# First self attention of a decoder: next batch's rows turned in the tail of the softmax loop, output projection in three rounded products

## What is computed

```python
x = _layernorm(x + _L0_attn_ref(x, Wq, bq, Wk, bk, Wv, bv, Wo, bo), axis=-1)

def _L0_attn_ref(x, Wq, bq, Wk, bk, Wv, bv, Wo, bo):
    q, k, v = (to_heads(x @ W + b) for W, b in ((Wq, bq), (Wk, bk), (Wv, bv)))   # 8 heads of 64
    scores = jnp.einsum('bdsh,bdth->bdst', q, k) / SCALE
    weights = jax.nn.softmax(scores, axis=-1)
    feats = jnp.einsum('bdst,bdth->bdsh', weights, v)
    return feats @ Wo + bo
```

## Time and profile before

| | |
|---|---|
| median of 3 executions | 2917.49 us (2911.3 to 2918.1) |
| profiled execution | 2918.93 us |
| its span, first to last instruction | 2917.2 us |
| PE busy | 2683.2 us, 92% of the span |
| DVE, ACT, POOL busy | 1798.4, 1422.5, 288.5 us |
| mean granted TensorE clock | 0.974 of full speed |
| first self attention | up to 477.9 us, where the next stage's first transpose starts |

### The profile page before, as it was taken

How to read it: one execution, slowest core, us unless ns; L and a number is a source line. 1 busy time by engine, 2 the same in 40 slices (tenths; PEclk the granted TensorE clock), 3 DMA queues, 4 the chain that set the end, 5 groups by cost and what they waited for, 6 DMA issues and landing times. The chain is left out here.

```text
span 2917.2 us, 40519 instructions
## 1 busy us (share of the span) xinstructions
PE 2683.2 (92%) x12686; PEld 1671.8 (57%) x12686; DVE 1798.4 (62%) x3459; ACT 1422.5 (49%) x2981; POOL 288.5 (10%) x397
## 2 busy tenths in 40 slices
PE   8998998979799995999999999997999999997888
PEld 4454554444388872677677777775545454533443
DVE  5665674644443335656756756754777777874676
ACT  5453553422033332355454553653677676764554
POOL 0230003001521104000000000001110101000000
PEclk9999999989899998999999999999999999998999
DMA  4395105531587762523223223211000000002000
GB/s 151 73 114 159 43 14 166 200 131 60 164 264 239 238 210 58 195 78 126 81 102 110 73 102 116 72 73 58 6 5 6 5 6 2 2 2 88 8 22 30
DMA packets 114166, 266.24 MB, mean 91 GB/s; under 512 B 14464, under 2 KB 37008, under 8 KB 113200
## 3 DMA queue, kind: packets, MB, share of 16 engines
q1 hardware_dynamic: 97152, 211.16, 22.0%
q0 software_dynamic: 16816, 52.64, 8.1%
HBM read 208.97 MB, written 58.48 MB: 92 GB/s over the span
## 5 line engine op out<-in xcount | busy, mean ns | idle before, releaser
L2451 DVE TENSOR_REDUCE x_neg_max<-bank 128x1 f32<-128x512 f32 x512 | 327.4, 684 | 95.9 <-PE bank L2296 95.6
L2403 ACT ACTIVATE x_weights<-bank 128x512 f32<-128x512 f32 x512 | 279.1, 600 | 127.0 <-PE bank L2307 122.2
L1830 ACT ACTIVATE a_probs<-bank,a_neg_max 128x128 f32<-128x128 f32 (+3 forms) x256 | 136.2, 532 | 201.2 <-DVE a_neg_max L1924 197.0
L1730 PE MATMUL bank<-a_x_high,a_weights 128*128 128x512 f32 x640 | 218.4, 404 | 7.8 <-DVE a_x_low L1854 2.3
L109 PEld LDWEIGHTS bank<-all_ident,a_probs 128*128 128x128 f32 x1200 | 151.5, 140 | 84.3 <-issue 44.7
L109 PE MATMUL bank<-all_ident,a_probs 128*128 128x128 f32 x1200 | 193.4, 273 | 2.2 <-ACT a_probs_t L1822 2.2
L1822 ACT COPY a_probs_t<-bank 128x128 f32<-128x128 f32 (+3 forms) x256 | 107.6, 420 | 144.1 <-PE bank L109 143.9
L1765 PE MATMUL bank<-a_k_cols,a_q_cols 128*128 128x128 f32 (+3 forms) x512 | 176.7, 434 | 0.5 <-DVE a_q_cols L1873 0.3
L1794 PE MATMUL bank<-a_wo,a_att_high 128*128 128x512 f32 x512 | 162.2, 398 | 4.7 <-DVE a_q_cols L1873 2.9
L1455 DVE TENSOR_TENSOR moe_acc<-bank,moe_acc 128x512 f32 x79 | 54.7, 692 | 170.4 <-PE bank L1121 170.2
L1110 PE MATMUL bank<-moe_gh_cols,moe_item 128*128 128x256 f32 x632 | 152.0, 384 | 4.1 <-DMA moe_item<-moe_items 3.5
(11 more groups left out here) (406 smaller groups left out, 5394.3 us busy)
## 6 DMA issues: line engine op xcount, KB each, us to landing
a_weights<-split_qkv SPq DMA_DIRECT2D x80, 512.0 KB, 3.6
moe_item<-moe_items SPq DMA_DIRECT2D x79, 257.0 KB, 3.9
moe_item<-moe_items SPq DMA_DIRECT2D x79, 256.0 KB, 3.9
a_wo<-split_out SPq DMA_DIRECT2D x8, 2048.0 KB, 8.0
a_wo<-split_out SPq DMA_DIRECT2D x16, 1024.0 KB, 10.3
split_qkv<-x_qkv_parts SPq DMA_DIRECT2D x12, 1024.0 KB, 5.1
moe_items<-in_L_ffn_e_w POOLq DMA_DIRECT2D x40, 256.0 KB, 34.5
split_out<-a_turned SPq DMA_DIRECT2D x8, 1024.0 KB, 4.0
```

The source lines that it names most:

```text
L1730: last = pe.matmul(mm[g % 2], weight[:, k, :], x[:, k, :], start=n == 0, stop=n == 3 * KD - 1)
L1830: act.activation(probs[:, n % SLOTS, 0:t], sc[n % 4][:, 0:t], ACT.Exp, bias=neg_max[:, n:n + 1], accum_out=row_sum[:, n:n + 1]).then_inc(s ...
L2403: act.activation(weights[:, chunk % 2, k, :], weight_banks[slot % 2], ACT.Exp).then_inc(s.weight.free, 1)
L2451: dve.tensor_reduce(neg_max[:, g % 2, j, h:h + 1], score_banks[slot % 3], AX.X, ALU.max, negate=True) \
```

## The change

Two things change in `self_attention_0`.

The next batch's rows are turned within the softmax loop, at i = 38 to 41, one tile of rows each. SP loads `x_rows` earlier for that, after the second pair's values (which read the tile for the last time), and the two loads into `whole` and `high` now come behind it in SP's order. ACT copies the turned rows to `x_cols` at the end of its softmax loop. The last batch has no next one, so its body is written out separately behind a loop over three batches; the first batch's rows are turned ahead of the loop.

The output projection takes three products of rounded parts for each float32 one: high x high, high x low, low x high. The weights are split once, by two POOL instructions at the start (`wo` is loaded into `turned[0]` and `wo_high`, `wo_low` made of it). `feats` is split in each batch: ACT's copy from the bank makes `feats_high`, DVE subtracts it from the same bank for `feats_low`, both in the tile `q_parts`, which is free by then. ACT and DVE may write `turned` first when POOL has split the weights (the starting count of `out_stored` now comes from POOL).

```diff
-    X0, Q0, F0 = 0, NT, NT + TILES
-    SC, TA, TV, MM = F0 + NT, TILES // 2, TILES // 2, 3 * KD + 2 * GROUPS + NT
+    NEXT_X = TILES + 6
+    Q0, SC = NT, TILES + 2 * NT
+    TA, TV, MM = TILES // 2, TILES // 2, 3 * KD + 2 * GROUPS + NT
...
-        feats, feats_t = sb("feats", [P, NT, D]), x_cols
+        wo = turned[0]
+        feats_high, feats_low = q_parts[:, 0:KD, :], q_parts[:, KD:2 * KD, :]
+        feats = sb("feats", [P, NT, D])
...
-            with sp.Fori(1, B) as b:
-                load_out(b - 1)
+            with sp.Fori(0, B - 1) as b:
                 sp.wait_ge(x_tok_loaded, 16)
-                sp.wait_ge(s.mm.full, b * MM - NT)
-                sp.dma_start(x_rows[:], m.x_tok[:, bass.ds(b * NT, NT), :]).then_inc(s.x_loaded, 16)
-                store_out(b - 1)
+                sp.wait_ge(s.mm.full, b * MM + 3 * KD + 3)
+                sp.dma_start(x_rows[:], m.x_tok[:, bass.ds(b * NT + NT, NT), :]).then_inc(s.x_loaded, 16)
+                load_out(b)
+                store_out(b)
...
+                    if not last_one and 0 <= i - NEXT_X < NT:
+                        if i == NEXT_X:
+                            pe.wait_ge(s.x_loaded, b * 16 + 32)
+                        turn_x(i - NEXT_X, b * SC + Q0 + TILES)
...
-                pe.wait_ge(w_out, 32)
+                pe.wait_ge(s.wo_split, 1)
...
                     for c in range(KD):
-                        last = pe.matmul(mm[g % 2], feats_t[:, c, j * P:(j + 1) * P], wo[:, c, :],
-                                         start=c == 0, stop=c == KD - 1)
+                        for part, weight in ((feats_high, wo_high), (feats_high, wo_low), (feats_low, wo_high)):
+                            last = pe.matmul(mm[g % 2], part[:, c, j * P:(j + 1) * P], weight[:, c, :], start=n == 0, stop=n == 3 * KD - 1)
+                            n += 1
...
+                if not last_one:
+                    keep_x(b * SC + Q0 + TILES)
                 for j in range(NT):
                     act.wait_ge(s.sc.full, b * SC + F0 + j + 1)
-                    act.copy(feats_t[:, :, j * P:(j + 1) * P], blocks_of(sc[j], KD)).then_inc(s.sc.free, 1)
+                    act.copy(feats_high[:, :, j * P:(j + 1) * P], blocks_of(sc[j], KD)).then_inc(s.feats_high_ready, 1)
...
+                bias_rows(0, 2)
                 for j in range(NT):
-                    x = m.x_tok[:, b * NT + j, :]
-                    dve.tensor_tensor(x, x, bo_row[:], ALU.add)
+                    tile = slice(j * P, (j + 1) * P)
+                    dve.wait_ge(s.feats_high_ready, b * NT + j + 1)
+                    dve.tensor_tensor(feats_low[:, :, tile], blocks_of(sc[j], KD), feats_high[:, :, tile].bitcast(F32),
+                                      ALU.subtract).then_inc(s.sc.free, 1)
+                bias_rows(2, NT)
...
+            pool.wait_ge(w_out, 32)
+            pool.tensor_copy(wo_high[:], wo[:]).then_inc(s.wo_high_made, 1)
+            pool.wait_ge(s.wo_high_made, 1)
+            pool.tensor_tensor(wo_low[:], wo[:], wo_high[:].bitcast(F32), ALU.subtract).then_inc(s.wo_split, 1)
+            pool.wait_ge(s.wo_split, 1)
+            pool.sem_inc(s.out_stored, 16)
             layernorm_rstd(pool, st, 0, m, s)
```

More of the change, by code:

```diff
@@ L152, in self_attention_0 @@
     PARTS = 2 * KD
-    X0, Q0, F0 = 0, NT, NT + TILES
-    SC, TA, TV, MM = F0 + NT, TILES // 2, TILES // 2, 3 * KD + 2 * GROUPS + NT
+    NEXT_X = TILES + 6
+    Q0, SC = NT, TILES + 2 * NT
+    TA, TV, MM = TILES // 2, TILES // 2, 3 * KD + 2 * GROUPS + NT
     with ExitStack() as ctx:
         sb, sem = allocator(nc, ctx, "a0")
-        wq, wk, wv, wo = (sb(n, [P, KD, D]) for n in ("wq", "wk", "wv", "wo"))
+        wq, wk, wv = (sb(n, [P, KD, D]) for n in ("wq", "wk", "wv"))
+        wo_high, wo_low = sb("wo_high", [P, KD, D], F32R), sb("wo_low", [P, KD, D], F32R)
         bq_col, bk_col = sb("bq_col", [P, KD]), sb("bk_col", [P, KD])
@@ L179, in self_attention_0 @@
         s.zeros_made = sem("zeros_made")
+        s.wo_high_made, s.wo_split, s.feats_high_ready = sem("wo_high_made"), sem("wo_split"), sem("feats_high_ready")
         s.out_rows_in, s.out_high, s.out_low, s.out_stored = (sem(n) for n in ("out_rows_in", "out_high", "out_low", "out_stored"))
@@ L225, in _, with turn_x, batch @@
                 pe.sem_inc(ring.free, ring.size)
-            pe.sem_inc(s.out_stored, 16)
-            with pe.Fori(0, B) as b:
-                pe.wait_ge(s.x_loaded, b * 16 + 16)
-                for j in range(NT):
-                    pe.wait_ge(s.sc.free, b * SC + X0 + j + 1)
-                    turn_tile(pe, sc[j], x_rows[:, j, :], m.ident[:], KD).then_inc(s.sc.full, 1)
+            def turn_x(j, use):
+                pe.wait_ge(s.sc.free, use + j + 1)
+                turn_tile(pe, sc[j], x_rows[:, j, :], m.ident[:], KD).then_inc(s.sc.full, 1)
+            def batch(b, last_one):
+                F0 = NT + TILES if last_one else TILES + 2 * NT
                 pe.wait_ge(s.sc.free, b * SC + s.sc.size + Q0)
@@ L295, in _, with keep_x, batch @@
                     pe.wait_ge(s.mm.free, b * MM + g + 1)
+                    n = 0
                     for c in range(KD):
-                        last = pe.matmul(mm[g % 2], feats_t[:, c, j * P:(j + 1) * P], wo[:, c, :],
-                                         start=c == 0, stop=c == KD - 1)
+                        for part, weight in ((feats_high, wo_high), (feats_high, wo_low), (feats_low, wo_high)):
+                            last = pe.matmul(mm[g % 2], part[:, c, j * P:(j + 1) * P], weight[:, c, :], start=n == 0, stop=n == 3 * KD - 1)
+                            n += 1
                     last.then_inc(s.mm.full, 1)
+            pe.wait_ge(s.x_loaded, 16)
+            for j in range(NT):
+                turn_x(j, 0)
+            with pe.Fori(0, B - 1) as b:
+                batch(b, False)
+            batch(B - 1, True)
         @block.scalar
         def _(act):
-            with act.Fori(0, B) as b:
+            def keep_x(use):
                 for j in range(NT):
-                    act.wait_ge(s.sc.full, b * SC + X0 + j + 1)
+                    act.wait_ge(s.sc.full, use + j + 1)
                     act.copy(x_cols[:, :, j * P:(j + 1) * P], blocks_of(sc[j], KD)).then_inc(s.sc.free, 1)
+            def batch(b, last_one):
+                F0 = NT + TILES if last_one else TILES + 2 * NT
                 for g in range(PARTS):
@@ L341, in _ @@
                     act.copy(out_parts[u][:, :, 0, :], out_rows[u]).then_inc(s.out_high, 1)
+            keep_x(0)
+            with act.Fori(0, B - 1) as b:
+                batch(b, False)
+            batch(B - 1, True)
         @block.vector
@@ L401, in _, with bias_rows @@
                 dve.wait_ge(x_tok_loaded, 16)
-                for j in range(NT):
-                    x = m.x_tok[:, b * NT + j, :]
-                    dve.tensor_tensor(x, x, bo_row[:], ALU.add)
+                def bias_rows(first, end):
+                    for j in range(first, end):
+                        x = m.x_tok[:, b * NT + j, :]
+                        dve.tensor_tensor(x, x, bo_row[:], ALU.add)
+                bias_rows(0, 2)
+                for j in range(NT):
+                    tile = slice(j * P, (j + 1) * P)
[3 more added lines that the diff above has]
+                bias_rows(2, NT)
                 dve.drain()
```

## The result

The changed kernel took 2926.2 us (median of 8 runs, 2921.4 to 2934.7) where the kernel before took 2917.2 on the same chip (8 runs, 2911.3 to 2920.0). The ratio is 1.004, 95% interval 1.0027 to 1.0052: slower by 0.4%. In a later set of runs the ratio was 1.0009 (0.9997 to 1.0021), where no change can be told. The profiled execution took 2925.99, with a span of 2924.2, which is 7.0 more than before. The forecast was 2919.5, in a range of 2908 to 2929.

What follows compares the result with a forecast made beforehand. PE, busy for 92% of the span, was taken as the bound. Projection -11.4, feats split +1.2, turning -2.5, x_rows load +7.7 and POOL's split +7.0 summed to +2.0: 2920.9 profiled, 2919.5 median, range 2908 to 2929.

Steps and rivals of the forecast that it cites:

- Split on POOL: Start of batch 0: POOL's rounding and subtraction of the output weights hold DVE's low key parts, cost 2.5 + 4.5 = 7.0.
- Wait on x_rows: Batch 1: the earlier load meets the expert packing, lands in 24 us, and PE stands 11 (6.6 to 22.6).
- The lower clock: Batch 1, behind the wait for x_rows: PE restarts at its lower clock, cost 1.6.
- Rival B: Batch 1: x_rows lands in time, queues sharing engines packet by packet, some 10 us; 2917, at best 2909; chance 0.13.
- Projection: Output projection: 48 rounded matmuls in 10.88 us instead of 13.73, gain 2.85 per batch, 11.4 in four.
- Turning: Batch boundaries: 2.93 us disappears, transposes cost 2.1 in the softmax tail; gain 0.85 per boundary, 2.5 in three.
- the lateness of DVE: After each boundary: DVE some 1.6 us behind PE but catching up before the keys; cost nothing, up to 0.3 per boundary.
- The wait for the low part of feats: Ahead of the output projection: PE waits 0.3 per batch for DVE's subtraction, 1.2 in four.
- Sum: Whole kernel: -11.4 + 1.2 - 2.5 + 7.7 + 7.0 = +2.0 us, giving 2919.5 for the median.
- Later stages unchanged: Stages after the first self attention: lengths claimed unchanged in the profile after.
- its own sign (3 us): Stages other than the first self attention: forecast called wrong if one changes by more than 3 us.

Runs made afterwards that it cites:

- set 2: Second group of follow-up runs, on its own chip: changed kernel again (1.0009 of the kernel before), packing late (1.0079), packing and split late (1.0053), projection only (0.9967).
- set 3: Third group, on its own chip: kernel before again (2917.2 us), turning only (1.0054), feats parts in k (2928.8 us), packing meant in two halves (1.0021).
- sets 1 and 2: First two groups of follow-up runs, each on its own chip, kernel before 2930.6 and 2908.6 us; the first had late split, PE written out, both, both with clearing late.

## Why the prediction was right, and where not

The terms inside the first self attention were the right ones, and most came out a little worse than forecast. Two things were luck. The change cost 9.0 us by the medians, the forecast was 2.0, and it was the wide range (2908 to 2929) that held 2926.2. And the landing of 24 us was right in size by a wrong account of where the time goes.

- *Split on POOL*: forecast 7.0, measured 5.8. The rounding took 2.15 (1.89 in other traces) where I took 2.5; the estimate of 1.8 to 3.1 by the Trainium skill, "GPSIMD Engine Reference", section "Elementwise — side-by-side cycle accounting", holds it. The two POOL instructions filled 7.06, as forecast, but 1.54 of DVE's 2.79 was done by the time POOL ended: its first subtraction had begun 0.28 before POOL, and its second came through behind POOL's rounding. In set 2 the first projection ran late and POOL's work stood partly beside other work: 2.71 of waiting instead of 4.29.
- *Wait on x_rows*: forecast a landing of 24 and a wait of 11; measured 25.3 and 12.33, then 22.4 to 27.5 and 9.3 to 14.4 in the others. The forecast took the rate of 0.40 MB in 10 us for the whole way. The trace has 10.2 us without a packet and then the megabyte in 15, so the size came out right by the wrong way. The lower clock behind it cost 2.2 instead of 1.6. Rival B is out in every trace in which the packing ran; what keeps it out is above all the delay of the first packet, more than the share of the queues that the earlier trace rows suggested: had the first packet come after 1.2 us, the same 15 behind it would leave a wait of some 3 us (an estimate from these times).
- *Projection*: forecast 10.88 by the pace of another stage, measured 11.30: 1.7 us less gain in four batches. The pace of the earlier trace rows was not that of this place.
- *Turning*: the way from the transposes of `products` to those of `feats` grew from 5.89 to 8.32, so 2.43 in the tail where I took 2.1, and 0.5 gained per boundary instead of 0.85. In front of the softmax loop 0.35 more went, the lateness of DVE that the sum had at nothing (up to 0.3). The wait for the low part of feats was 0.25, forecast 0.3.
- *Sum*: per quiet batch the gain was 2.35 (111.73 against 114.1) instead of 3.4; batch 1 lost 7.6 instead of 4.3; the stage 4.8 instead of 2.0. The last batch gained 3.44, part of it because the kernel before had 3.4 us at the lower clock there (from 455.6).
- *Later stages unchanged*: this part failed, and by its own sign (3 us). The cross attention came out 5.8 longer in the changed kernel's first trace, 141.1 from its first transposes to the first matmul of the next part, and 5.5 of that lie in its first block of x (29.3 against 23.9, rows above). All 14 traces sort by it. Where the rows are turned between the batches (the kernel before twice, the projection alone) that block takes 22.2 to 23.9; of the eleven where they are turned in the tail one has 22.3, the changed kernel again, and the others have 25.2 to 29.3, each with more time at the lower clock and some with longer waits on the first loads. So this looks like a part of the price of the new order, and it would cover most of what the stage's 4.8 leave of the 9.0. How the order of the first stage brings it about was not tested and stays open.
- *Missed*: that POOL's clearing DMA, which I had as a limit under rival B only, can be next in line in the plain forecast too. Where the packing drains at 260 and not at 249, the changed kernel waits for the DMA twice. Between its two traces the end of the stage moved from 482.7 to 494.0, 11.3 us, as much as the largest term of my sum. How much of that the kernel before pays on the same chip was not measured.

## What to carry to other kernels

Before a load is moved earlier, look at what fills the DMA engines at its new time, and how long a load issued then waits for its first packet: here 5 us became 25, 10 of them before the first packet, and the wait was longer than all that the new order saved. A short instruction must not stand on a queue behind a DMA issue that waits for room; moving one root of a layer norm ahead of one such issue was worth about 15 us in one set, more than this change cost. Work for POOL that reads SBUF belongs beside stretches in which DVE reads PSUM. And a change in one stage is to be read in the first 30 us of the next as well.

## What the runs showed of the hardware

The same packing took 113 to 120 us in the first two traces and in set 3, and 131 to 135 in sets 1 and 2, from the root before it to the DMA behind it. With it running, a load on the hardware queue moved its first packet 9.4 to 12.7 us after its issue in six traces of the early load, against 1.2 on idle engines. Two POOL instructions held one DVE subtraction each until 0.55 us after their end. The first query projection took 13.97 or 15.7 to 16.2 us, by whether its first matmuls started 0.43 or 0.85 us apart. And a program written out for PE stood 10.43 us with no semaphore to wait for that the profile shows, while the packing ran.
